# First cross attention of a two-layer decoder: context weights in four loads, values and fill placed later on VectorE, first score tiles moved among the projections

## The reference, cut to what matters

```python
def _L0_xattn_ref(q, k, v, mask, Wq, bq, Wk, bk, Wv, bv, Wo, bo):
    def heads(x, W, bias):
        y = x @ W.T + bias
        return y.reshape(b, -1, H, DK).transpose(0, 2, 1, 3)
    qh, kh, vh = heads(q, Wq, bq), heads(k, Wk, bk), heads(v, Wv, bv)
    scores = jnp.einsum('bhqd,bhkd->bhqk', qh, kh) / math.sqrt(DK)
    scores = jnp.where(mask == 0, jnp.float32(-1000000000.0), scores)
    weights = jax.nn.softmax(scores, axis=-1)
    out = jnp.einsum('bhqk,bhkd->bhqd', weights, vh)
    out = out.transpose(0, 2, 1, 3).reshape(b, -1, H * DK)
    return out @ Wo.T + bo
x = x + _L0_xattn_ref(_layernorm(x, axis=-1), ctx_1024, ctx_1024, mask, ...)
```

## Time and profile before

| | |
|---|---|
| median of 3 runs | 1968.27 us (1967.85 to 1970.39) |
| the profiled execution, its time | 1966.19 us |
| its span in the profile | 1964.5 us |
| TensorE busy | 1697.7 us (86%) |
| VectorE busy | 1243.5 us (63%) |
| first cross attention | about 0 to 232 us of the span |
| second cross attention begins | at 1383 us |

### The profile page before, as it was taken

How to read it: one execution, slowest core, us unless ns; L and a number is a source line. 1 busy time by engine, 2 the same in 40 slices (tenths; PEclk the granted TensorE clock), 3 DMA queues, 4 the chain that set the end, 5 groups by cost and what they waited for, 6 DMA issues and landing times. The chain is left out here.

```text
span 1964.5 us, 30055 instructions
## 1 busy us (share of the span) xinstructions
PE 1697.7 (86%) x10579; PEld 801.6 (41%) x10580; DVE 1243.5 (63%) x2131; ACT 964.8 (49%) x1803; POOL 580.0 (30%) x637
## 2 busy tenths in 40 slices
PE   6899799899999999999997984999289985149996
PEld 4466454222222222222222663776145652035564
DVE  6454458788888888888880694665755535661221
ACT  3423254588888888888886221444383322002110
POOL 5200063342221112111212153666562002022433
PEclk9999999899999999999999986999599997659998
DMA  5000069532222232222200622221400004311543
GB/s 145 1 2 2 20 187 320 188 63 40 40 40 39 52 62 42 40 39 40 40 2 14 238 72 83 64 66 55 134 1 1 2 1 163 108 34 29 142 98 33
DMA packets 112773, 134.51 MB, mean 68 GB/s; under 512 B 18576, under 2 KB 88592, under 8 KB 112368
## 3 DMA queue, kind: packets, MB, share of 16 engines
q1 hardware_dynamic: 101920, 114.20, 21.5%
q0 software_dynamic: 9552, 17.83, 3.8%
q10 hardware_dynamic: 1152, 0.54, 0.1%
HBM read 78.47 MB, written 53.93 MB: 67 GB/s over the span
## 5 line engine op out<-in xcount | busy, mean ns | idle before, releaser
L1070 DVE TENSOR_REDUCE sa_mhalf<-sa_a 128x2 f32<-128x1024 f32 x512 | 604.3, 1221 | 84.4 <-PE sa_a L1282 82.5
L1215 ACT ACTIVATE sa_e<-sa_b 128x512 f32<-128x512 f32 x683 | 383.7, 601 | 76.9 <-PE sa_b L1315 76.9
L1325 PE MATMUL sa_b2o<-sa_e,sa_v 128*17 128x512 f32 x2048 | 269.7, 598 | 0.0
L1215 ACT ACTIVATE sa_e<-sa_b2o 128x512 f32<-128x512 f32 x341 | 205.2, 602 | 40.6 <-PE sa_b2o L1315 40.6
L1315 PE MATMUL sa_b<-sa_q,sa_k 112*128 112x512 bf16 x468 | 163.4, 388 | 2.7 <-ACT sa_e L1215 2.7
L1018 POOL TENSOR_TENSOR sa_rden<-sa_o_rows,sa_minus_one 128x16 f32<-128x16 f32 x32 | 93.1, 2909 | 178.1 <-ACT sa_o_rows L1198 178.1
L234 DVE TENSOR_REDUCE xa_mx<-xa_rows 128x16 f32<-128x1024 f32 x64 | 78.3, 1224 | 92.9 <-PE xa_rows L603 92.6
L1282 PE MATMUL sa_a<-sa_k,sa_q 48*128 48x512 bf16 x704 | 113.4, 389 | 13.2 <-DVE sa_mhalf L1070 13.2
L1007 POOL CAST sa_negm<-sa_neg 16x128 bf16<-16x128 f32 x32 | 9.4, 293 | 348.7 <-issue 338.9
L478 ACT ACTIVATE xa_pT<-xa_cols 128x1024 f32<-128x1024 f32 x64 | 62.1, 1022 | 82.5 <-PE xa_cols L635 82.5
L1315 PEld LDWEIGHTS sa_b<-sa_q,sa_k 112*128 112x128 bf16 x468 | 40.7, 97 | 151.3 <-ACT sa_e L1215 130.1
(11 more groups left out here) (345 smaller groups left out, 2979.8 us busy)
## 6 DMA issues: line engine op xcount, KB each, us to landing
k_parts<-sa_parts SPq DMA_DIRECT2D x96, 128.0 KB
tc_w<-in_L_ffn_W SPq DMA_DIRECT2D x24, 512.0 KB
sa_q<-q_parts SPq DMA_DIRECT2D x44, 192.0 KB, 5.5
sa_k<-k_parts SPq DMA_DIRECT2D x44, 192.0 KB, 5.8
q_parts<-sa_parts SPq DMA_DIRECT2D x16, 384.0 KB
ex_xg<-expert_in SPq DMA_DIRECT2D x39, 132.0 KB
v_groups<-sp_vt SPq DMA_DIRECT2D x8, 544.0 KB, 5.9
sa_v<-v_groups SPq DMA_DIRECT2D x16, 272.0 KB, 7.6
```

The source lines that it names most:

```text
L1070: nc.vector.tensor_reduce(mhalf[a % 2][:, half, head:head + PAIRED + 1:PAIRED, t], aps[a_slot(use)][:], axis=X, op=ALU.max).then_inc(a_use ...
L1215: nc.scalar.activation(ex[(KT * n + kt) % (LAG + 1)][:, head], bps[use % 3], ACT.Exp, scale=SCALE).then_inc(b_used, 1)
L1325: last = nc.tensor.matmul(ops[32 * head:32 * head + VW], vs[s][:, kt, head], ex[(KT * n + kt) % (LAG + 1)][:, head], start=(kt == 0), stop ...
```

## The change

`Context.issue` now loads each weight matrix by itself: that of the keys first, then the context, the values' matrix, the queries', `bqk` and `bv`; each group has its own semaphore. The output matrix and `bo` are loaded by a new function, `issue_output`, which the first cross attention calls behind all of x and the mask, and the second right behind `issue`. The mask is loaded before chunk 4 of x instead of after chunk 7. TensorE waits for keys, values and queries one after another, and for the rest before `attend`. VectorE places the key bias, the values and the fill at later points. ScalarE waits for the key bias later. Three score tiles of chunk 0 stand among the projections of chunks 5, 6 and 7 instead of two.

```diff
     def issue(self, sp):
         w = self.w
-        loads = [(self.wts[:], w["wts"].rearrange("f (k p) n -> p f k n", p=P))]
-        loads += [(self.ctxT[:, k, :, twice, :], w["ctxT"][k * P:(k + 1) * P]) for twice in range(2) for k in range(HALVES)]
-        loads += [(self.bqk[:], w["bqk"]), (self.bv[:], w["bv"].partition_broadcast(P)),
-                  (self.bo[:], w["bo"].partition_broadcast(P))]
-        for dst, source in loads:
+
+        def weights(f):
+            return self.wts[:, f], w["wts"][f].rearrange("(k p) n -> p k n", p=P)
+
+        def load(semaphore, *loads):
+            for dst, source in loads:
+                sp.dma_start(dst, source).then_inc(semaphore, 16)
+            return 16 * len(loads)
+
+        self.keys_count = load(self.keys_loaded, weights(1), *[(self.ctxT[:, k, :, twice, :], w["ctxT"][k * P:(k + 1) * P])
+                                                               for twice in range(2) for k in range(HALVES)])
+        self.values_count = load(self.values_loaded, weights(2))
+        self.queries_count = load(self.queries_loaded, weights(0))
+        self.count = load(self.loaded, (self.bqk[:], w["bqk"]), (self.bv[:], w["bv"].partition_broadcast(P)))
+        self.issued = True
+
+    def issue_output(self, sp):
+        w = self.w
+        for dst, source in ((self.wts[:, 3], w["wts"][3].rearrange("(k p) n -> p k n", p=P)),
+                            (self.bo[:], w["bo"].partition_broadcast(P))):
             sp.dma_start(dst, source).then_inc(self.loaded, 16)
-        self.issued, self.count = True, 16 * len(loads)
+        self.whole = self.count + 32
...
                         if c == 0:
                             context.issue(sp)
-                    sp.dma_start(mask_i[:], mask.rearrange("(t p) k -> p t k", p=P)).then_inc(mask_loaded, 16)
+                        if c == 3:
+                            sp.dma_start(mask_i[:], mask.rearrange("(t p) k -> p t k", p=P)).then_inc(mask_loaded, 16)
+                    context.issue_output(sp)
...
                     moments(1)
-                    place_key_bias()
                     for c in range(CHUNKS):
                         if c >= 1:
                             normalize_x(c)
-                        if c == 0:
-                            place_values()
                         if c + 2 < CHUNKS:
                             moments(c + 2)
+                        if c == 0:
+                            place_key_bias()
                         if c == 2:
+                            place_values()
+                        if c == 3:
                             place_fill()
...
-                pool.wait_ge(context.loaded, context.count)
+                pool.wait_ge(context.loaded, context.whole)
...
-                    act.wait_ge(kbias_made, 1)
...
+                    if c == 0:
+                        act.wait_ge(kbias_made, 1)
...
-                pe.wait_ge(context.loaded, context.count)
+                pe.wait_ge(context.keys_loaded, context.keys_count)
...
+                pe.wait_ge(context.values_loaded, context.values_count)
...
+                pe.wait_ge(context.queries_loaded, context.queries_count)
...
-                        if c >= CHUNKS - 2:
+                        if c >= CHUNKS - 3:
                             pe.wait_ge(qT_ready, HALVES)
-                            scores(0, c - (CHUNKS - 2))
-                    scores(0, 2)
+                            scores(0, c - (CHUNKS - 3))
                     scores(0, 3)
...
+                pe.wait_ge(context.loaded, context.whole)
```

More of the change, by code:

```diff
@@ L85, in __init__ @@
         self.w, self.loaded, self.issued = w, kit.sem("loaded"), False
+        self.keys_loaded, self.values_loaded, self.queries_loaded = (kit.sem(f"{n}_loaded") for n in ("keys", "values", "queries"))
         self.wts = kit.sb("wts", [P, 4, HALVES, D])
```

## The result

The changed kernel takes 1959.47 us in the median of 5 runs (1955.42 to 1961.88), the kernel before 1968.44 (1967.85 to 1970.39): 9.0 us less, ratio 0.995 with a 95% interval of 0.9936 to 0.9965. The profiled execution, with 1961.88, was the slowest of the five.

The account below looks back on a forecast made before the run. TensorE was taken as the bound from t2 (chunk 2's transposes) on, after idling before t1; attend's start counted. 7.5 (t4) + 1.4 (tile) = 8.9 us off 1966.19 gives 1957.3, 1959.4 with the median 2.1 higher; range 1956.0 to 1964.5.

Parts of the forecast that it names:

- t4: TensorE's transposes of normalised chunk 4 in the first cross attention: start at 33.6 instead of 41.07, 7.5 us sooner.
- Loads: With fewer context loads ahead, chunk 1 of x arrives 2.0 us sooner, at 13.0; TensorE's 1.88 us wait before the keys goes.
- late-chunk rival: Chunk 1 or 4 comes late: weight pieces load at 106 instead of 347 GB/s, gain 3.8 us, 1964.5; chance 0.14.
- t1: TensorE's transposes of normalised chunk 1: start at 19.0 instead of 25.23, right behind the values, without waiting.
- VectorE's chain: VectorE's moments, normalisations, values and fill from chunk 1's arrival: 1.5 us wait for chunk 4, n3 (normalisation 3) ending at 27.9.
- t3: TensorE's transposes of normalised chunk 3: wanted at 27.6, nearly met, a wait of 0.3 us for VectorE.
- n7 under the bias: VectorE's normalisation of chunk 7 beside GpSimd's output bias: takes 8.6 us, ends at 48.3, covered by 1.1 us.
- The rival in which the bias takes the gain: GpSimd's bias also slows n6 (normalisation 6) to 8.6 us; gain only 2.8 us, 1965.5; chance 0.08.
- Tile: Moving one score tile from behind the projections to among them saves TensorE 1.4 us; bounds 0 to 1.4.
- Second cross attention: Keys made sooner there, but TensorE still waits for ScalarE: gain 0, bounds 0.3 us to either side.
- A: Arrival time of chunk 1 of x, from which VectorE's order is timed: forecast 13.0, bounds 12.3 to 15.0.
- all behind it moves with it: Claim that everything after the start of attend (74.07 us in the kernel before) shifts by the same amount as that start.

Follow-up runs that it names:

- first series: The changed kernel's original five runs beside the kernel before; median 1959.47 us, ratio 0.995.
- mask-last kernel: The changed kernel with the mask loaded behind all of x again; 1960.96 us, ratio 0.9952 to the kernel before.
- shapes-moved kernel: The kernel with the mask loaded last, with GpSimd's selector and shares made behind rstd of chunk 0 and the spread behind rstd of chunk 7; 1957.41 us.
- two-tiles kernel: The changed kernel with two score tiles among the projections instead of three; 1963.32 us, ratio 0.9971 to the kernel before.
- order with the tile: The kernel before with its old loads, but VectorE's new order and three score tiles among the projections; 1962.28 us, ratio 0.9964.
- loads alone: The changed kernel with VectorE's old order and two score tiles among the projections; median of twelve 1968.91 us, ratio 1.000 to the kernel before.
- shift-first kernel: The loads alone, with VectorE making the last chunk's shift ahead of a score tile's maximum in the second cross attention; 1966.84 us, ratio 0.9987.
- kernels with the filler: 32 identity transposes added on TensorE between the values and t1: in the loads alone, 1961.46 us; in the kernel before, 1964.39 us.

## Why the prediction was right

**Its sum.** To attend 8.9 us were forecast and 8.4 came: t4 7.2 sooner (7.5 forecast), and from t4 to attend 1.2 less (1.4 forecast). The medians give 9.0 in the first series and 8.2 in the second. That the forecast met the first median to 0.1 us is luck, since the series differ by more.

**Loads.** Chunk 1 was forecast at 13.0 and measured at 13.21, 1.8 sooner than before. In the eleven profiles with the new loads it came between 12.76 and 14.21, in the three with the old ones between 15.04 and 16.38. The keys' wait went, with keys at 11.50. The late-chunk rival, to which the prediction ties the rule of the Trainium skill, "DMA: Bandwidth & Descriptors", section Bandwidth, on transfers of 1 MiB or more, did not come: from 5 to 13 us the DMA moved 218 to 377 GB/s in every microsecond, not 106.

**t1.** 19.0 was forecast, 18.16 measured: the keys took 3.20 to the values' start instead of 3.58, and the values 3.46 instead of 3.75. Why is not shown; in the other profiles with the new loads, all without an idle stretch in front of the keys, the first of the two ranges from 2.30 to 3.42. It did not help further on, as VectorE was the bound.

**VectorE's chain.** For chunk 4 a wait of 1.5 was forecast, 1.30 measured, and the mask-last kernel shows it to be the mask's cost. t4 was forecast at 33.6 and measured at 33.88. Inside, t3 waited 1.91 where 0.3 was forecast. Of the 1.6 between them, 0.7 come from TensorE being there sooner (26.94 instead of 27.6) and 0.9 from n3, which ended at 28.80 instead of 27.9, most of it since n3 took 2.23 beside GpSimd's spread, where the prediction took 1.5. The shapes-moved kernel shows this contention. It was not in the forecast, and the rows from which a normalisation was priced hold some of it (1.68 at 32.45, while GpSimd made rstd).

**n7 under the bias.** 8.6 forecast, 9.54 measured; cover 1.1 forecast, 0.5 left. It held in the changed kernel; without the tile in front, t7 waited 0.65. The rival in which the bias takes the gain was near: n6 ended at 39.55, the bias began at 39.74. The row from which the prediction could have seen this is n6 of the kernel before, which took 3.44 (at 42.25) with its end under the bias.

**Tile.** 1.4 was forecast. The two-tiles kernel shows 2.1 behind t4, the 1.4 of the wait and 0.65 that the tile saves t7. Against the kernel before only 1.2 are left, because t7 did not wait there.

**Second cross attention.** 0 was forecast, with 0.3 to either side. From its start to the last stage it took 240.81 us before, 240.98 and 240.73 in the two profiles of the changed kernel.

**What was missed.** The prediction gives one sum for loads and order and does not say what each is worth. The order with the tile brings 7.0 of the 8.2 to 9.0, the loads without them 0.3 in the median, though 2.2 to 3.3 at attend. With the new order the loads move A, and the mask's wait of 1.3 takes most of that back. And "all behind it moves with it" does not hold from profile to profile: in the first profile of the changed kernel 4.1 of 8.4 us were gone by the end (1.6 in the last projection of the stage, 1.9 in the last stage), in the second 3.0 of 7.8. The medians show the whole gain since the kernel before is, in the median, 2 to 3 us above its one profile (1966.19), and the changed kernel is at or below its two. That the mechanism up to attend was right is shown; that the median follows it this closely is in part luck.

**What stays open.** Why the loads alone took 4 to 12.5 us more than in the first profile in the other eleven executions of that series. One slow execution was taken apart; the shift-first kernel does not settle it. The kernel before is not free of it either, with times from 1965.0 to 1973.59 beside the loads alone. The changed kernel seems to be: none of its eleven executions is above 1965.12. Whether part of its gain is that it falls less often into the slower executions, as the kernels with the filler suggest, is a rival to the account by attend alone that the runs do not rule out.

## What to carry to other kernels

Ask of each late operation what the engine in front of it does meanwhile: values placed at 19 to 22 us, which no matmul read before 88.78, stood ahead of a normalisation for which TensorE waited, and moving them was worth more than faster loads. Price a removed idle stretch of TensorE with the slow clock behind it, and a moved VectorE operation with what GpSimd does at that time. A small operation on which another engine depends is safer ahead of the wait that can push it under a long one (ahead of the maximum, the shift took 0.17 us in its profile); what that is worth in time was not settled here. Compare stages between two profiles before the end of the span is believed.

## What the runs showed of the hardware

In one execution, a fall of the clock by 1.7 us grew to 5.5 through two VectorE operations that landed under a GpSimd operation and a second fall of the clock behind them; a 128x4 operation took 2.32 us there instead of 0.15. Executions of one kernel ranged over 12.5 us (1961.56 to 1974.06), more than the effect studied; attend held to 1.1 us in its three profiled executions, whose times ranged over 8.1. And behind a 1 MB transfer of 4096 pieces of 256 bytes (the mask) SP's next issue lasted 8.67 us in the changed kernel, from 9.60, and 7.80 in the mask-last kernel, where it is another transfer:

```profile
9.60 8.67 SPq L188 DMA_DIRECT2D x_x<-in_x  x1
```

In the changed kernel that issue is the load of chunk 4, for which VectorE then waits. It ends at 18.27, and around its end the DMA engines ran partly empty, at 120 GB/s from 18 to 20, where they moved 217 just before and 373 just after:

```profile
18.00:20.00 2.00, 2.00 (x13) 1.00 0.62 120
```

So the wait of 1.30 for chunk 4 may hold more than the mask's own transfer; how much of it is the held issue was not tried.
